# State-space layer: a chunk's steps in another order on four engines, projection and convolution in halves, output projection in its own bank

## What is computed

```python
xz = x @ W_in
x_in, z = jnp.split(xz, 2, axis=-1)
...
x_in = _silu(x_conv)                     # causal convolution, 4 taps
dbc = x_in @ W_xproj
dt = jax.nn.softplus(dbc[..., :DT_RANK] @ W_dt + b_dt)
...
def step(state, inp):
    x_t, dt_t, B_t, C_t = inp
    dA = jnp.exp(jnp.clip(dt_t[:, :, None] * A[None], -10.0, 10.0))
    dB = dt_t[:, :, None] * B_t[:, None, :]
    state = jnp.clip(state * dA + x_t[:, :, None] * dB, -10.0, 10.0)
    y_t = jnp.einsum('bdn,bn->bd', state, C_t) + D * x_t
    return (state, y_t)
...
y = y * _silu(z)
return y @ W_out
```

## Time and profile before

| | us |
|---|---|
| median of three runs | 4619.2 (4618.07 to 4622.37) |
| profiled execution, its own time | 4624.27 |
| its span | 4622.4 |
| PE busy | 3818.7 (83%) |
| DVE busy | 2992.2 (65%) |
| ACT busy | 2502.0 (54%) |
| POOL busy | 2258.6 (49%) |
| mean granted clock of TensorE | 0.911 |

### The profile page before, as it was taken

One profiled execution on the slowest core, in us unless ns is written; L12 is line 12 of the kernel. 1 busy time (PEld: TensorE's weight loads), 2 busy tenths in 40 slices (PEclk: granted clock), 3 DMA queues, 4 the chain that ended last, 5 costly groups with the idle time before them and its releaser, 6 DMA issues.

```text
span 4622.4 us, 72113 instructions
## 1 busy us (share of the span) xinstructions
PE 3818.7 (83%) x22840; PEld 2878.8 (62%) x22840; DVE 2992.2 (65%) x5611; ACT 2502.0 (54%) x6473; POOL 2258.6 (49%) x1253
## 2 busy tenths in 40 slices
PE   4888888888888857999588888888888888888886
PEld 2444444444444436777477777777777777777776
DVE  3445454554555322222398888888988888988987
ACT  1433434443434422333477776777768677776774
POOL 4233233333323220000377776767777677777774
PEclk8889999998998878999798999999899998999998
DMA  2322223322322216666222221222222222222221
GB/s 84 95 74 82 92 79 94 95 86 75 96 80 75 73 44 206 206 210 204 77 83 72 74 84 67 81 77 82 72 77 83 75 74 81 74 78 74 81 77 39
DMA packets 268587, 419.76 MB, mean 91 GB/s; under 512 B 60245, under 2 KB 232662, under 8 KB 245656
## 3 DMA queue, kind: packets, MB, share of 16 engines
q1 hardware_dynamic: 255896, 380.98, 25.5%
q0 software_dynamic: 12288, 33.57, 2.1%
HBM read 330.56 MB, written 83.10 MB: 89 GB/s over the span
## 4 chain that ended last, share of the span: by engine, by line
PE 14%; POOL 12%; ACT 9%; DVE 9%; issue 7%; DMA 1%; DVEq 0%; SPq 0%; ACTq 0%; POOLq 0%
POOL m_ub L1532 10%; ACT m_dA L1650 6%; PE m_Y L1900 6%; PE m_Y L1910 3%; DVE m_PR L1754 2%; DVE m_PR L1762 2%; DVE m_S L1754 2%; DVE m_S L1762 2%; POOL m_yg L1542 1%; PE m_Y L1913 1%; PE m_F L1873 1%; PE m_F L1854 1%; DVE m_ub L1739 1%; PE m_F L1865 1%; POOL m_dtx L1511 1%
## 5 line engine op out<-in xcount | busy, mean ns | idle before, releaser
L1532 POOL TENSOR_TENSOR m_ub<-m_Bb,m_dtx 128x2048 f32<-128x2048 f32 x256 | 1156.8, 4543 | 503.9 <-PE m_Y L1900 497.5
L1650 ACT ACTIVATE m_dA<-m_dt,m_a_neg 128x128 f32<-128x128 f32 x4096 | 1210.0, 389 | 27.2 <-DVE m_S L1762 23.2
L1900 PE MATMUL m_Y<-m_ub,m_ident 128*128 128x128 f32 x8192 | 1029.7, 291 | 207.7 <-DVE m_ub L1739 205.3
L1900 PEld LDWEIGHTS m_Y<-m_ub,m_ident 128*128 128x128 f32 x8192 | 1010.6, 206 | 217.4 <-DVE m_ub L1739 213.6
L534 ACT ACTIVATE f_pt<-f_X 128x512 f32<-128x512 f32 (+1 forms) x704 | 371.5, 554 | 720.6 <-PE f_X L822 690.2
L609 DVE TENSOR_REDUCE f_nm<-f_Y 128x1 f32<-128x512 f32 (+3 forms) x896 | 433.3, 530 | 361.9 <-PE f_Y L816 357.9
L1754 DVE SCALAR_TENSOR_TENSOR m_PR<-m_dA,m_S 128x512 f32<-128x512 f32 x512 | 355.8, 695 | 213.5 <-ACT m_dA L1650 84.4
L815 PE MATMUL f_Y<-f_kst,f_qst 96*128 96x512 bf16 (+3 forms) x1024 | 283.4, 332 | 109.3 <-DVE f_nm L609 92.0
L1754 DVE SCALAR_TENSOR_TENSOR m_S<-m_dA,m_PR 128x512 f32<-128x512 f32 x512 | 354.8, 693 | 12.0
L1762 DVE CUSTOM_DVE_ANT_1 m_PR<-m_PR,m_ub 128x512 f32<-128x512 f32 x512 | 353.0, 689 | 0.2 <-DVE m_PR L1754 0.2
L1762 DVE CUSTOM_DVE_ANT_1 m_S<-m_S,m_ub 128x512 f32<-128x512 f32 x512 | 353.0, 689 | 0.0
(11 more groups left out here) (241 smaller groups left out, 6644.2 us busy)
## 6 DMA issues: line engine op xcount, KB each, us to landing
m_Bb<-m_bc_dram SPq DMA_DIRECT2D x64, 1024.0 KB, 4.7
m_Cb<-m_bc_dram SPq DMA_DIRECT2D x64, 1024.0 KB, 4.7
f_parts_dram<-f_parts SPq DMA_DIRECT2D x32, 768.0 KB, 4.5
f_kst<-f_parts_dram SPq DMA_DIRECT2D x192, 128.0 KB, 2.6
f_qst<-f_parts_dram SPq DMA_DIRECT2D x192, 128.0 KB, 2.6
e_rows<-sorted_rows SPq DMA_DIRECT2D x70, 256.0 KB, 2.7
e_wg<-Wg SPq DMA_DIRECT2D x70, 256.0 KB, 2.9
e_wu<-Wu SPq DMA_DIRECT2D x70, 256.0 KB, 3.9
```

The costliest lines, as they stand in the source:

```text
L1532: pool.tensor_tensor(ub[:, h, i, :, :], Bb[:, s, :, :], dtx[:, par, m, None, s * SN:(s + 1) * SN].to_broadcast([P, NST, SN]), ALU.mult).th ...
L1650: last = act.activation(dA[:, h, i, n, :], dtt[:, par, m, s * SN:(s + 1) * SN], ACT.Exp, scale=a_neg[:, m, n:n + 1])
L1900: last = pe.matmul(Y[:, i * SN:(i + 1) * SN], ident[:, :], ub[:, h, i, n, :], start=False, stop=(n == NST - 1), skip_group_check=True)
```

## The change

- SyncE: `load_x` is issued for one chunk further ahead, in the middle of `spread_bc`, between the loads of its two halves.
- ScalarE: `normalise(c+2)` stands first in the body, `evac_T(c+2)` in front of `decays(c, 2)`, `softplus(c+1)` behind it; `evac_x` and `tanh_z` are woven into one `evac_xz`, upper half of the channels first.
- VectorE: `stats`, both `silu_x`, `add_res` and `log_rest` have other slots.
- TensorE: `dbc(c+1)` and `transposes(c+2)` go ahead of the output projection of chunk c - 1; the input projection is split in `project_a` behind `nsum(c, 0)` and `project_b` behind `nsum(c, 1)`, the convolution in one half behind `project_b` and one behind `nsum(c, 2)`. The transposes go to bank F0 instead of F2, the output projection to F2 instead of Y.

```diff
             for s in range(NSUB):
+                if s == NSUB - 1 and ahead is not None:
+                    load_x(ahead)
                 held(u_ready[2 * s + 1], 2 * c)
                 sp.dma_start(Bb[:, s, :, :], bc_dram[s:s + 1, 0, :, :].to_broadcast([P, NST, SN])).then_inc(b_loaded[s], 16)
                 held(sc_unit[2 * s + 1], c)
...
 
         def chunk(c, par, rows_ahead=True):
-            if rows_ahead:
-                load_x(c + 2)
             store(c - 1)
             load_res(c)
             load_info(c + 1, 1 - par)
-            spread_bc(c + 1)
+            spread_bc(c + 1, c + 3 if rows_ahead else None)
...
             act.wait_ge(xz_done, 4 * c)
-            act.activation(xnT[:, :, :], F[2][:, :, :], ACT.Copy).then_inc(xnT_ready, 1)
...
+        def evac_xz(c):
...
             for i in range(2):
-                act.wait_ge(xz_done, 4 * c + i + 1)
-                act.activation(xpad[:, 2 * i:2 * i + 2, HALO:HALO + CN], F[1 + i][:, :, :], ACT.Copy).then_inc(xpad_ready, 1)
-
-        def tanh_z(c):
-            for i in range(2):
-                act.wait_ge(xz_done, 4 * c + 3 + i)
+                hx = 1 - i
+                act.wait_ge(xz_done, 4 * c + 2 * i + 1)
+                act.activation(xpad[:, 2 * hx:2 * hx + 2, HALO:HALO + CN], F[1 + hx][:, :, :], ACT.Copy).then_inc(xpad_ready, 1)
+                act.wait_ge(xz_done, 4 * c + 2 * i + 2)
                 act.wait_ge(zs_ready, c)
                 act.activation(th_z[:, 2 * i:2 * i + 2, :], F[(3 + i) % 4][:, :, :], ACT.Tanh, scale=0.5).then_inc(thz_ready, 1)
                 act.wait_ge(sp_sub, c)
@@ -1608,9 +1605,10 @@
 
         def tanh_x(c):
             for i in range(2):
+                hx = 1 - i
                 act.wait_ge(conv_done, 2 * c + i + 1)
                 act.wait_ge(x2_ready, 2 * c)
-                act.activation(th_x[:, 2 * i:2 * i + 2, :], F[1 + i][:, :, :], ACT.Tanh, scale=0.5).then_inc(thx_ready, 1)
+                act.activation(th_x[:, 2 * hx:2 * hx + 2, :], F[1 + hx][:, :, :], ACT.Tanh, scale=0.5).then_inc(thx_ready, 1)
 
         def evac_dbc(c):
             act.wait_ge(dbc_done, c + 1)
...
         def body(c, par, first, last):
+            if has(c + 2):
+                normalise(c + 2)
             if not last:
                 evac_dbc(c + 1)
-                softplus(c + 1)
             if has(c + 2):
-                normalise(c + 2)
+                evac_T(c + 2)
             decays(c, par, 2)
             if not last:
+                softplus(c + 1)
                 ln(c + 1)
-                if has(c + 2):
-                    evac_T(c + 2)
             weigh(c, par)
             decays(c, par, 3)
+            if has(c + 2):
+                evac_xz(c + 2)
             if not last:
-                if has(c + 2):
-                    evac_x(c + 2)
-                    tanh_z(c + 2)
                 decays(c + 1, 1 - par, 0)
                 if has(c + 2):
                     tanh_x(c + 2)
@@ -1715,11 +1710,11 @@
                 dve.sem_inc(taken)
...
-            dve.tensor_tensor(ot[:, :, :], Y[:, :].rearrange("p (j d) -> p j d", j=TT), res[:, :, :], ALU.add).then_inc(ot_done, 1)
+            dve.tensor_tensor(ot[:, :, :], F[2][:, :, :], res[:, :, :], ALU.add).then_inc(ot_done, 1)
...
             slots = [dict() for _ in range(NU)]
             if not first:
                 slots[0][5] = lambda: gate_y(c - 1, 1 - par, NU - 1)
-                slots[1][0] = lambda: add_res(c - 1)
+                slots[1][1] = lambda: add_res(c - 1)
             for u in range(1, NU):
                 slots[u][6] = lambda u=u: gate_y(c, par, u - 1)
             if not last:
-                slots[0][6] = lambda: silu_x(c + 1, 1 - par, [0])
-                slots[0][7] = lambda: silu_x(c + 1, 1 - par, [1])
-                slots[1][7] = lambda: log_rest(c + 1)
+                slots[0][3] = lambda: silu_x(c + 1, 1 - par, [1])
+                slots[0][4] = lambda: silu_x(c + 1, 1 - par, [0])
+                slots[2][0] = lambda: log_rest(c + 1)
             if has(c + 2):
-                slots[0][3] = lambda: stats(c + 2)
+                slots[0][2] = lambda: stats(c + 2)
...
         def transposes(c):
             pe.wait_ge(xn_done, TT * (c + 1))
-            pe.wait_ge(x2_ready, 2 * c)
+            if not isinstance(c, int) or c > 0:
+                pe.wait_ge(z_copied, 2 * c)
             for k in range(KM):
                 for j in range(TT):
-                    last = pe.transpose(F[2][:, k, j * P:(j + 1) * P], xn[:, j, k * P:(k + 1) * P], ident[:, :])
+                    last = pe.transpose(F[0][:, k, j * P:(j + 1) * P], xn[:, j, k * P:(k + 1) * P], ident[:, :])
             last.then_inc(xT_done, 1)
 
-        def project(c):
+        def project(c, i):
+            for m in range(2):
+                blk = 2 * i + m
+                for k in range(KM):
+                    last = pe.matmul(F[(1 + i) % 4][:, m, :], w_in[:, k, blk * P:(blk + 1) * P], xnT[:, k, :],
+                                     start=(k == 0), stop=(k == KM - 1))
+            last.then_inc(xz_done, 1)
+
+        def project_a(c):
             pe.wait_ge(xnT_ready, c + 1)
-            for i in range(4):
-                if i == 0:
-                    pe.wait_ge(sp_low, c)
-                if i == 1:
-                    pe.wait_ge(x2_ready, 2 * c)
-                if i == 2:
-                    pe.wait_ge(bcrow_ready, c)
-                    pe.wait_ge(dtin_ready, c)
-                for m in range(2):
-                    blk = 2 * i + m
-                    for k in range(KM):
-                        last = pe.matmul(F[(1 + i) % 4][:, m, :], w_in[:, k, blk * P:(blk + 1) * P], xnT[:, k, :],
-                                         start=(k == 0), stop=(k == KM - 1))
-                last.then_inc(xz_done, 1)
-
-        def conv(c):
-            for i in range(2):
-                pe.wait_ge(xpad_ready, 2 * (c + 1))
-                for j in range(2):
-                    m = 2 * i + j
-                    pe.matmul(F[1 + i][:, j, :], b_cv[RANK:RANK + 1, m * P:(m + 1) * P], dt_in[RANK:RANK + 1, :], start=True, stop=False)
-                    for k in range(TAPS):
-                        last = pe.matmul(F[1 + i][:, j, :], cv_diag[:, k * MI + m, :],
-                                         xpad[:, m, k * BATCH:k * BATCH + CN], start=False, stop=(k == TAPS - 1))
-                last.then_inc(conv_done, 1)
+            pe.wait_ge(x2_ready, 2 * c)
+            if not isinstance(c, int) or c >= 3:
+                pe.wait_ge(ot_done, c - 2)
+            project(c, 1)
+            pe.wait_ge(bcrow_ready, c)
+            pe.wait_ge(dtin_ready, c)
+            project(c, 2)
+
+        def project_b(c):
+            pe.wait_ge(xnT_ready, c + 1)
+            pe.wait_ge(sp_low, c)
+            project(c, 0)
+            project(c, 3)
+
+        def conv(c, i):
+            pe.wait_ge(xpad_ready, 2 * c + (1 - i) + 1)
+            for j in range(2):
+                m = 2 * i + j
+                pe.matmul(F[1 + i][:, j, :], b_cv[RANK:RANK + 1, m * P:(m + 1) * P], dt_in[RANK:RANK + 1, :], start=True, stop=False)
+                for k in range(TAPS):
+                    last = pe.matmul(F[1 + i][:, j, :], cv_diag[:, k * MI + m, :],
+                                     xpad[:, m, k * BATCH:k * BATCH + CN], start=False, stop=(k == TAPS - 1))
+            last.then_inc(conv_done, 1)
 
...
         def dbc(c):
             pe.wait_ge(z_copied, 2 * c + 1)
-            for m in range(MI):
-                pe.wait_ge(x2_ready, 2 * c + m // 2 + 1)
+            for q in range(MI):
+                m = (q + 2) % MI
+                pe.wait_ge(x2_ready, 2 * c + q // 2 + 1)
                 last = pe.matmul(F[3][0:RANK + 2 * NST, 0, :], w_xp[:, m, :], x2[:, ipar[0], m, :],
-                                 start=(m == 0), stop=(m == MI - 1))
+                                 start=(q == 0), stop=(q == MI - 1))
             last.then_inc(dbc_done, 1)
...
         def dt_proj(c):
+            if has(c + 1):
+                pe.wait_ge(xnT_ready, c + 2)
...
-            if u > 0:
+            if u > 0 or not isinstance(c, int) or c > 0:
                 pe.wait_ge(yz_done, NU * c + u)
-            else:
-                pe.wait_ge(ot_done, c)
...
+            pe.wait_ge(ot_done, c)
             for j in range(TT):
                 for m in range(MI):
-                    pe.matmul(Y[:, j * DM:(j + 1) * DM], yz[:, m, j * P:(j + 1) * P], w_out[:, m, :],
+                    pe.matmul(F[2][:, j, :], yz[:, m, j * P:(j + 1) * P], w_out[:, m, :],
                               start=(m == 0), stop=False)
                 for k in range(TOPK):
-                    last = pe.matmul(Y[:, j * DM:(j + 1) * DM], wdiag[:, k, j, :], yg[:, k, j, :],
+                    last = pe.matmul(F[2][:, j, :], wdiag[:, k, j, :], yg[:, k, j, :],
                                      start=False, stop=(k == TOPK - 1))
             last.then_inc(outp_done, 1)
 
```

(49 more changed lines are left out.)

## The result

The changed kernel takes 4662.89 us (median of 4 runs, 4651.88 to 4673.60) against 4618.64 before (4 runs): a ratio of 1.0111, 95% interval 1.0070 to 1.0151. That is 44 us slower, where 75 had been forecast.

A forecast was written before the change was run, and what follows sets the result against it. The prediction took a ring of VectorE, TensorE's sums and GpSimd's inputs to bound the kernel; 2.57 us more a chunk over 29 chunks, +74.5 on the profiled 4624.3, gave 4699, median 4694; range 4605 to 4735.

The forecast's parts named there:

- The queue it named: Output projection, `dt_proj` and unit 0's sum now queue behind a 9 us GpSimd block, through `rstd_of`, `normalise` and the transposes.
- its signs: Expected in the trace: `m_xn` just behind `m_shift`, output projection at clock 0.50, VectorE waiting 3 to 7 us before unit 2.
- The chain at full clock: From VectorE's start of unit 0 to its start of unit 2, without slow matmuls: 38.0 us, against 38.2 before.
- The second part of a chunk: From the start of unit 2 to the next unit 0: 34.6 us with the loop's branch behind it, 33.3 without.
- The clock term: Idle TensorE slows matmuls: output projection loses 2.5 us a chunk, the sum of unit 3 2.26 behind the branch.
- The sum of unit 3: On TensorE early in a chunk: 2.26 us lost behind the branch after 3.5 to 3.8 idle, none otherwise after 2.3.
- The sum: Two chunks added up, 40.5 + 34.6 + 42.8 + 33.3 = 151.2 us, or 75.6 a chunk, 2.57 more than before.
- 0.2% for what a measurement can tell: For the whole kernel, a difference of 0.2% (9 us) was taken as about what a measurement can tell.
- The clock stays up: Rival: TensorE loses no clock before the output projection or sum of unit 3; 71.5 us a chunk, 4575 us, chance 0.18.
- Slow at every start: Rival: output projection loses 2.98 and unit 3's sum is slow in both chunks; 77.5 a chunk, 4749 us, chance 0.10.
- Costed at nothing: Taken as free: output projection's own bank, earlier `load_x`, `add_res` losing VectorE 3.9 us under cover, prologue and tail.
- over some 3 us: The deciding point for the clock: whether TensorE idles over some 3 us before the transposes; 4.3 us was expected.

The follow-up runs named there:

- filled kernel: The changed kernel with TensorE products nobody reads added, 9 ahead of the sum of unit 3 and 15 ahead of the transposes: 4594.85 us, ratio 0.9956 to before.
- both cures: The changed kernel with `rstd_of` ahead of unit 1's inputs on GpSimd and 9 unread products ahead of the sum of unit 3: 4477.41 us, ratio 0.9718 to before.
- the third filling: The kernel with both cures, plus 3 more unread products on TensorE ahead of each half of `dbc`: 4484.55 us, ratio 0.9730 to the kernel before.

## Why the prediction was right, point by point

- **The direction and the mechanism**, right. The queue it named (inputs of unit 1, `rstd_of`, `normalise`, transposes, output projection, `dt_proj`, sum, inputs of unit 2) is what the trace shows, link by link, and the run with `rstd_of` first, with its counter-test in the kernel before, shows that the queue is real and worth 5.2 us a chunk. The filled kernel shows the other part, the clock, worth 2.8. Taking away either turns the loss of 2.0 into a gain, so the loss needs both, as the prediction had it. Of its signs one came out smaller: VectorE waited 2.5 to 2.7 in front of unit 2, not 3 to 7, since it had already lost 1.9 in front of `silu_x` and 3.1 for `add_res`.
- **The chain at full clock**, 38.0: right. The filled kernel, in a pair of chunks with the granted clock at 1.00 in both places, measured 38.1 and 37.9.
- **The second part of a chunk**, 34.6 and 33.3: measured 34.5 and 32.8. The 0.5 came with the sum of unit 1: it was slow, as assumed, but took 8.76 from its start to the next step's (3261.00 to 3269.76) where the prediction had taken the 9.32 of before.
- **The clock term**, right in kind, mis-sized in both halves. "I take 2.5 lost" for the output projection: it took 6.20 and 6.84 (3312.05 to 3318.89 in the next chunk) instead of 5.18, and the transposes 0.91 instead of 0.60, so 1.3 and 2.0. The sum of unit 3: 2.26 had been taken behind the branch and nothing without it ("2.3 idle, no loss taken"); measured 5.64 to the products (3219.79 to 3225.43) instead of 3.82, 1.8 in both kinds of chunk. That made 41.2 and 41.6 out of 42.8 and 40.5: 82.8 in the place of the 83.3 expected. That the two come so near is luck: 1.6 too much behind the branch and 1.1 too little without it cancel. The step that was wrong is that 2.3 us of idle time would leave the sum of unit 3 at full clock. The idle time in front of the transposes was near the 4.3 expected (4.1) by luck as well: `dbc` and the transposes both came 2 later than reckoned.
- **The sum**, 151.2 for two chunks: measured 150.1. Of the missing 30 us, 0.54 a chunk x 29 = 16 is the clock term and the second part. The rest is the distance between 59 us by the loop, 55 by the state-space part of the profiles and 44 by the medians. It stays open, since the interval of the medians reaches from 32 to 70. The prediction's 0.2% for what a measurement can tell was too fine: the interval is 0.4% to either side.
- **The rivals.** "The clock stays up" was priced at 4575 and measured, when it was brought about, at 4594.85: the mechanism holds, but the kernel as changed is not in that case. "Slow at every start" had the sum of unit 3 right (slow in both chunks behind 3.80 and 2.24 us idle) and too high a price, 77.5 against 75.06: the output projection lost less than its 2.98, the sum 1.8 instead of 2.26, and the second part came out shorter.
- **Costed at nothing**: own bank and earlier load, both confirmed, by one run each. `add_res` waits 3.1 to 3.3 (3.9 forecast) under the cover of a late unit 2, as described. The wait in front of `silu_x`, 1.8 to 1.9 behind the slow sum, was not foreseen. It costs nothing in the change, but it became a bound once `rstd_of` was moved, and removing it was worth another 0.9 us a chunk.

By the Trainium skill, "TensorE: Matmul & The Clock Gate", section "What's actually happening", the ramp penalty is, for modelling, under 1% of a typical kernel's span. Here the clock was worth 2.8 of 75.06 us a chunk, 68 of 4663 us or 1.5% of the whole; that is more than the change's whole effect, and the measurement decides. There the Trainium skill has the ramp at a kernel's start in view; here the clock fell again in every chunk.

## What to carry to other kernels

An in-order queue that is handed a step early inherits everything that step waits for: before moving a step ahead on one engine, follow its inputs back through the lists of the others, down to the engine that the change leaves alone. Here one unchanged line on GpSimd decided between 1.1% slower and 2.0% faster. And a step pulled out of a gap leaves the gap, so that what follows it on TensorE may start at the lower clock level: price that per start, in each chunk, from rows.

## What the runs showed of the hardware that was not expected

- The length of an idle stretch does not tell by itself whether the clock falls, and the prediction's "over some 3 us" does not hold. The sum of unit 3 took 9.04 in the change and 7.41 in the kernel with the output projection first, behind 2.24 us of idle TensorE each time; the sum of unit 1 took 9.04 with both cures and 7.41 with the third filling, behind 3.19 each time. In that order:

```profile
3293.84 9.04 PE L1903 MATMUL m_Y<-m_ub,m_ident 128*128 128x128 f32 x64 [2.24 <-DVE m_ub L1734]
3139.00 7.41 PE L1902 MATMUL m_Y<-m_ub,m_ident 128*128 128x128 f32 x64 [2.24 <-DVE m_ub L1733]
3092.07 9.04 PE L1904 MATMUL m_Y<-m_ub,m_ident 128*128 128x128 f32 x64 [3.19 <-DVE m_ub L1735]
3104.19 7.41 PE L1910 MATMUL m_Y<-m_ub,m_ident 128*128 128x128 f32 x64 [3.19 <-DVE m_ub L1735]
```

- The place where the clock fell moved with each filling: with the sum of unit 3 kept fast it fell in `dbc` and the output projection in some chunks; with those filled too, at the sum of unit 3 behind the branch. The one that was added last brought nothing (69.38 against 68.96 a chunk).
- At the end of the loop's body VectorE stands idle for 2.24 us or more with no releaser, once in two chunks. In the change the second part of a chunk took 34.5 with it and 32.8 without, so it costs about 1.7. That the branch is the cause is read from its place; no run tested it.
